# Convolution as 32x32 blocks on the array's diagonal, and router logits from four column tiles

## The reference

```python
xr = x @ in_proj_w.T
xs, res = jnp.split(xr, 2, axis=-1)
xc = conv_general_dilated(moveaxis(xs, 1, 2), conv_w, window_strides=(1,), padding=[(3, 0)],
                          feature_group_count=512)          # one 4-tap filter a channel
xs = silu(moveaxis(xc + conv_b[None, :, None], 2, 1))
dt, B, C = split(xs @ x_proj_w.T, ...)
delta = softplus(dt @ dt_proj_w.T + dt_proj_b)
y = selective_scan(xs, delta, -exp(A_log), B, C)            # h = exp(delta A) h + delta u B;  y = C h
x = x + ga * ((y * silu(res)) @ out_proj_w.T)
h = layernorm(x) * (1 + cb) + sb
s_raw = h @ Wg                                              # router logits, 8 a token
x = x + gb * moe(h, s_raw, Wl1, Wl2)
```

## Time and profile before

| | us |
|---|---|
| median of 3 runs | 2515.86 |
| lowest and highest | 2515.31, 2516.01 |
| span of the profiled execution | 2510.4 |
| mean granted TensorE clock in it | 0.902 |

### The profile page before, as it was taken

How to read it: one execution, slowest core, us unless ns; L and a number is a source line. 1 busy time by engine, 2 the same in 40 slices (tenths; PEclk the granted TensorE clock), 3 DMA queues, 4 the chain that set the end, 5 groups by cost and what they waited for, 6 DMA issues and landing times. The chain is left out here.

```text
span 2510.4 us, 31164 instructions
## 1 busy us (share of the span) xinstructions
PE 2181.1 (87%) x7664; PEld 1059.5 (42%) x7665; DVE 1929.5 (77%) x2060; ACT 1390.4 (55%) x2472; POOL 1955.0 (78%) x840
## 2 busy tenths in 40 slices
PE   8769998989989898999898988989857649999997
PEld 3214343443434343444343443434323335556654
DVE  2799899999999999989899999999897162222222
ACT  3666666667575766666666667576644232222221
POOL 1999889898989898989889898989897014555553
PEclk9878889898989898988989898989878869999999
DMA  5443242424232323434242424232321062222221
GB/s 155 129 112 96 73 102 66 100 71 112 79 94 73 97 76 95 107 85 102 73 102 67 101 69 114 80 92 77 91 68 39 26 208 77 85 84 82 87 85 45
DMA packets 149402, 224.40 MB, mean 89 GB/s; under 512 B 48227, under 2 KB 85617, under 8 KB 145138
## 3 DMA queue, kind: packets, MB, share of 16 engines
q1 hardware_dynamic: 135858, 182.44, 27.8%
q0 software_dynamic: 13376, 40.12, 5.1%
HBM read 99.48 MB, written 31.47 MB: 52 GB/s over the span
## 5 line engine op out<-in xcount | busy, mean ns | idle before, releaser
L1029 POOL TENSOR_TENSOR hs<-hs,c_rep 128x2048 f32<-128x2048 f32 x256 | 1154.8, 4532 | 41.3 <-ACT state L772 41.1
L869 DVE TENSOR_TENSOR_SCAN hs<-dA,state,hs 128x512 f32<-128x512 f32 x768 | 931.4, 1265 | 20.7 <-ACT dA L752 16.4
L752 ACT ACTIVATE dA<-d_rep,a 128x512 f32<-128x512 f32 x1024 | 688.8, 686 | 411.2 <-DVE hs L869 409.2
L1022 POOL TENSOR_TENSOR hs<-u_rep,b_rep 128x2048 f32<-128x2048 f32 x96 | 435.8, 4540 | 88.6 <-PE bank L516 88.5
L856 DVE TENSOR_TENSOR hs<-u_ps,b_rep 128x2048 f32<-128x2048 f32 x160 | 361.2, 2274 | 10.1 <-issue 5.1
L487 PE MATMUL bank<-n,w1s 128*128 128x512 f32 x512 | 269.0, 663 | 68.0 <-DVE delta L837 39.2
L869 DVE TENSOR_TENSOR_SCAN hs<-dA,hs 128x512 f32<-128x512 f32 x256 | 294.2, 1204 | 20.0 <-ACT dA L752 18.8
L516 PE MATMUL bank<-hs,spread 128*32 128x512 f32 x2048 | 280.4, 696 | 31.1 <-POOL hs L1029 27.0
L1414 DVE TENSOR_TENSOR hid<-z,sg 128x512 f32<-128x512 f32 x70 | 48.4, 692 | 298.2 <-ACT sg L1392 298.2
L1332 PE MATMUL z<-w1r,hT 128*128 x560 | 260.6, 608 | 3.5 <-issue 2.4
L445 PE MATMUL bank<-xin,w_in 128*128 128x512 f32 x512 | 246.3, 621 | 7.9 <-ACT xin L599 7.9
(11 more groups left out here) (174 smaller groups left out, 2566.3 us busy)
## 6 DMA issues: line engine op xcount, KB each, us to landing
d_rep<-delta SPq DMA_DIRECT2D x1024, 64.0 KB, 2.0
u_rep<-us SPq DMA_DIRECT2D x384, 64.0 KB, 2.0
b_rep<-bc_rows SPq DMA_DIRECT2D x64, 256.0 KB, 4.4
c_rep<-bc_rows SPq DMA_DIRECT2D x64, 256.0 KB, 7.8
xres<-in_x SPq DMA_DIRECT2D x16, 512.0 KB, 3.3
token_rows<-xpad SPq DMA_DIRECT2D x32, 256.0 KB, 2.4
token_rows<-xres SPq DMA_DIRECT2D x16, 512.0 KB, 2.9
xin<-in_x SPq DMA_DIRECT2D x15, 512.0 KB, 9.4
```

The source lines that it names most:

```text
L752: nc.scalar.activation(dA[:, u % ABANK, :], d_rep[:, q, :], ACT.Exp, scale=t["a"][:, u:u + 1]).then_inc(da_ready, 1)
L869: nc.vector.tensor_tensor_scan(hs[:, s % RING, g, :], dA[:, u % ABANK, :], hs[:, s % RING, g, :], state[:, u:u + 1] if m else 0.0, ALU.mul ...
L1022: nc.gpsimd.tensor_tensor(hs[:, s % RING], u_rep[:, i % UBUF, :].unsqueeze(1).to_broadcast([P, NG, T]), b_rep[:, par, :].rearrange("p (g t ...
L1029: nc.gpsimd.tensor_tensor(hs[:, s % RING, :, :], hs[:, s % RING, :, :], c_rep[:, par, :].rearrange("p (g t) -> p g t", g=NG), ALU.mult).th ...
```

## The change

The convolution no longer uses diagonal matrices of 128x128. Of a diagonal matrix only the 32x32 blocks on the diagonal are kept: `w_conv` becomes 32 columns wide, and each matmul has 32 rows and 32 columns. Tile position (32 r, 32 b) of the array takes rows 32 r of block b of `xpad` and writes partitions 32 b of bank r: a result bank then holds 32 channels of each of the four blocks, and the host permutes the weights behind it to that order (`held_by`). Two banks, r = j and j + 1, are computed at once: CV 0 does CV 0 and CV 1, CV 2 does CV 2 and CV 3, with 32 matmuls each (4 taps, 4 blocks, 2 rows of tiles), and both banks are taken first. CV 1 and CV 3 are empty on TensorE. All four blocks of `xs` are waited for. `conv_made` rises by one after the last matmul of each of the two banks, both at the end of the pair.

The logits get the router's weights, padded to 32 columns, as stationary operand, and `h2T` as the moving one, 128 columns for each token tile, with the four token tiles in four column tiles. The result, experts by tokens, is copied by ScalarE to `lgT` (item GL), turned by one transpose (item GT, on TensorE after B 0), and copied again to `lg` (GT in ScalarE's table, before B 1).

```diff
-            9: [(('GL', 0), -1), (('RB', 1), -1), (('SUM', 1), 0), (('B', 0), -1), (('B', 1), -1), ...
+            9: [(('GL', 0), -1), (('RB', 1), -1), (('SUM', 1), 0), (('B', 0), -1), (('GT', 0), -1), (('B', 1), -1), ...
-            10: [[(('E0', 0), 1), (('GL', 0), -1), (('L0', 0), 1), (('RB', 1), -1)], [], [(('B', 0), -1)], [(('B', 1), -1)]],
+            10: [[(('E0', 0), 1), (('GL', 0), -1), (('L0', 0), 1), (('RB', 1), -1)], [], [(('B', 0), -1)], [(('GT', 0), -1), (('B', 1), -1)]],
...
+                if kind == "CV":
+                    return convolve(j, c, f)
...
-                elif kind == "CV":
-                    pe.wait_ge(xs_ready, KI * f + j + 1)
-                    for k in range(KCONV):
-                        last = nc.tensor.matmul(ps_[:, :], t["w_conv"][:, j, k, :], xpad[:, j, k:k + T], start=(k == 0), stop=(k == KCONV - 1))
...
                 elif kind == "GL":
                     pe.wait_ge(h2T_ready, KD * f + KD)
-                    for tt in range(TT):
-                        for k in range(KD):
-                            last = nc.tensor.matmul(ps_[:, tt * NEXP:(tt + 1) * NEXP], h2T[:, k, tt * P:(tt + 1) * P], t["wg"][:, k, :],
-                                                    start=(k == 0), stop=(k == KD - 1))
+                    for k in range(KD):
+                        for tt in range(TT):
+                            last = nc.tensor.matmul(ps_[DS * tt:DS * tt + DS, 0:P], t["wg"][:, k, :], h2T[:, k, tt * P:(tt + 1) * P],
+                                                    start=(k == 0), stop=(k == KD - 1), skip_group_check=True, tile_position=(0, DS * tt))
+                elif kind == "GT":
+                    pe.wait_ge(lgT_ready, f + 1)
+                    last = nc.tensor.transpose(ps_[:, 0:P], lgT[:], t["ident"][:])
...
+            def convolve(j, c, f):
+
+                if j % 2:
+                    return
+                first = take_bank(pe, ("CV", j), c, f)
+                pe.sem_inc(held, 1)
+                second = take_bank(pe, ("CV", j + 1), c, f)
+                pe.sem_inc(held, 1)
+                pair = ((j, first), (j + 1, second))
+                hold(pe, xs_ready, KI * f + KI, held)
+                for k in range(KCONV):
+                    for b in range(KI):
+                        for r, ps_ in pair:
+                            rows = slice(DS * r, DS * r + DS)
+                            last = nc.tensor.matmul(ps_[DS * b:DS * b + DS, :], t["w_conv"][rows, b, k, :], xpad[rows, b, k:k + T],
+                                                    start=(k == 0), stop=(k == KCONV - 1), skip_group_check=True, tile_position=(DS * r, DS * b))
+                            if k == KCONV - 1 and b == KI - 1:
+                                last.then_inc(conv_made, 1)
...
                 elif kind == "GL":
+                    nc.scalar.activation(lgT[:], ps_[:, 0:P], ACT.Copy).then_inc(lgT_ready, 1)
+                elif kind == "GT":
                     if not (known(f) and f == 0):
                         act.wait_ge(logits_stored, 16 * f)
-                    nc.scalar.activation(lg[:], ps_[:, 0:TT * NEXP].rearrange("p (t e) -> p t e", t=TT), ACT.Copy).then_inc(logits_kept, 1)
+                    nc.scalar.activation(lg[:], ps_[:, 0:P].rearrange("p (t e) -> p t e", t=TT)[:, :, 0:NEXP], ACT.Copy).then_inc(logits_kept, 1)
...
-                    last = nc.vector.tensor_scalar(t["w_conv"][:, j, k, :], t["ident"][:], cw[:, j, k:k + 1], None, ALU.mult)
+                    last = nc.vector.tensor_scalar(t["w_conv"][:, j, k, :], t["gather"], cw[:, j, k:k + 1], None, ALU.mult)
```

More of the change, by code:

```diff
@@ L86, in fused_program @@
         hs = sb("hs", [P, RING, NG, T])
-        lg, gs = sb("lg", [P, TT, NEXP]), sb("gs", [P, 2, TT])
+        lg, lgT, gs = sb("lg", [P, TT, NEXP]), sb("lgT", [P, P]), sb("gs", [P, 2, TT])
         state = t["state"]
@@ L124, in fused_program @@
         logits_made, logits_kept, logits_stored = sem("logits_made"), sem("logits_kept"), sem("logits_stored")
+        lgT_made, lgT_ready = sem("lgT_made"), sem("lgT_ready")
         gate_in, gate_exp, gate_inv, gate_soft, gate_ready = sem("gate_in"), sem("gate_exp"), sem("gate_inv"), sem("gate_soft"), sem("gate_ready")
@@ L141, in fused_program @@
             8: [(('RS', 2), 1), (('RS', 3), 1), (('T2', 0), -1), (('T2', 1), -1), (('DT', 0), 1), (('DT', 1), 1), (('RB', 0), -1)],
-            9: [(('GL', 0), -1), (('RB', 1), -1), (('SUM', 1), 0), (('B', 0), -1), (('B', 1), -1), (('B', 2), -1), (('DB', 0), 1), (('B', 3), -1), (('DT', 2), 1)],
+            9: [(('GL', 0), -1), (('RB', 1), -1), (('SUM', 1), 0), (('B', 0), -1), (('GT', 0), -1), (('B', 1), -1), (('B', 2), -1), (('DB', 0), 1), (('B', 3), -1), (('DT', 2), 1)],
             10: [],
@@ L205, in fused_program @@
                  ("DT", 0), ("DT", 1), ("DB", 0), ("DT", 2), ("DT", 3), ("DB", 1), ("RS", 0), ("DB", 2), ("RS", 1), ("DB", 3), ("RS", 2), ("RS", 3)]
-        ACT_READS = ("T", "XS", "CV", "RS", "XP", "DT", "T2", "RB", "GL", "B")
+        ACT_READS = ("T", "XS", "CV", "RS", "XP", "DT", "T2", "RB", "GL", "GT", "B")
         made = {"T": turned, "XS": xs_made, "RS": res_made, "CV": conv_made, "XP": xdbl_made, "DT": dt_made, "DB": db_made, "SUM": y_ready, "OP": out_made,
-                "T2": turned2, "RB": back_made, "GL": logits_made, "B": b_made, "A": a_made, "Y": out2_made}
+                "T2": turned2, "RB": back_made, "GL": lgT_made, "GT": logits_made, "B": b_made, "A": a_made, "Y": out2_made}
         kept = {"T": hT_ready, "XS": xs_ready, "RS": res_pre, "CV": us_pre, "XP": xdbl_ready, "DT": abs_ready, "DB": delta_ready, "SUM": yg_ready, "OP": x1_ready,
-                "T2": h2T_ready, "RB": back_kept, "GL": logits_kept, "B": b_kept, "A": hid_ready, "Y": acc_ready}
+                "T2": h2T_ready, "RB": back_kept, "GL": lgT_ready, "GT": logits_kept, "B": b_kept, "A": hid_ready, "Y": acc_ready}
         many = {"T": KD, "XS": KI, "RS": KI, "CV": KI, "XP": 1, "DT": KI, "DB": KI, "SUM": KI, "OP": 2,
-                "T2": KD, "RB": 2, "GL": 1, "B": KI, "A": KI, "Y": 2}
+                "T2": KD, "RB": 2, "GL": 1, "GT": 1, "B": KI, "A": KI, "Y": 2}
         FRONT = ("T", "XS", "CV", "RS", "XP", "DT", "DB")
@@ L1437, in build @@
                 "w_in": sb("w_in", [P, KD, 2 * DI]), "w_x": sb("w_x", [P, KI, PROJ]), "w_dt": sb("w_dt", [DT_ROWS, DI]),
-                "w_out": sb("w_out", [P, KI, D]), "w_conv": sb("w_conv", [P, KI, KCONV, P]), "sa": sb("sa", [P, KD, BATCH]),
+                "w_out": sb("w_out", [P, KI, D]), "w_conv": sb("w_conv", [P, KI, KCONV, DS]), "sa": sb("sa", [P, KD, BATCH]),
                 "ca": sb("ca", [P, KD, BATCH]), "sb2": sb("sb2", [P, KD, BATCH]), "cb2": sb("cb2", [P, KD, BATCH]),
-                "w1s": sb("w1s", [P, KD, 2 * H]), "w2s": sb("w2s", [P, KI, D]), "wg": sb("wg", [P, KD, NEXP])}
+                "w1s": sb("w1s", [P, KD, 2 * H]), "w2s": sb("w2s", [P, KI, D]), "wg": sb("wg", [P, KD, DS])}
             fused_program(nc, ins, t, bc_dram, wout_dram, w2_dram, mod_dram, gb_dram, rows_dram, logits_dram)
@@ L1455, in laid_out @@
     c = np.ascontiguousarray
+    held_by = np.arange(DI).reshape(SPC, KI, DS).transpose(1, 0, 2).reshape(DI)
+    w_in = a["L0_attn_in_proj_w"].T
     return {
         "x": c(a["L0_attn_x"].reshape(BATCH * SEQ, D)),
[L1459 to L1464, removed]
+        "w_in": c(np.concatenate([w_in[:, :DI], w_in[:, DI + held_by]], axis=1)), "conv_w": c(a["L0_attn_conv_w"].reshape(KI, P, KCONV).transpose(1, 0, 2)),
+        "conv_b": c(a["L0_attn_conv_b"][held_by].reshape(KI, P).T),
+        "w_x": c(np.insert(a["L0_attn_x_proj_w"].T[held_by], DT_RANK, 0.0, axis=1)),
+        "w_dt": c(np.concatenate([a["L0_attn_dt_proj_w"].T, a["L0_attn_dt_proj_b"][None]])[:, held_by]),
+        "a_cols": c(a["L0_attn_A_log"][held_by].reshape(KI, SPC, DS, NF, NG).transpose(3, 2, 0, 1, 4).reshape(P, NSET * NG)),
+        "w_out": c(a["L0_attn_out_proj_w"].T[held_by]), "wg": c(np.pad(a["L0_ffn_Wg_DN"], ((0, 0), (0, DS - NEXP)))), "w1": c(a["L0_ffn_Wl1_ND2H"]), "w2": c(a["L0_ffn_Wl2_NHD"]),
         "c": c(a["L0_c"].reshape(BATCH, KD, P).transpose(2, 1, 0)), "wmod": c(a["L0_wmod"]),
```

## The result

| | before | after |
|---|---|---|
| median of the runs, us | 2515.14 (2510.93 to 2516.5) | 2519.18 (2517.29 to 2522.06) |
| ratio of the times | | 1.0021, 95% interval 1.0014 to 1.0029 |
| span of the profiled execution, us | 2510.4 | 2516.4 |
| mean granted TensorE clock in it | 0.902 | 0.874 |

What follows compares the result with a forecast made beforehand. VectorE's scan thread was taken to bound the kernel. Logits -28.5, second pair +49.5, prologue -4, tail -1.9 sum to +15.1 us; with span 2510.4 and 5.5 around it, 2531.0 us, range 2484 to 2556 (forecast's own range 2511 to 2552).

Steps and rivals of the forecast that it cites:

- Logits, chunks 1 to 15: Ahead of SUM 1: logits 1.2 us for 3.58, VectorE gains 1.9 us a chunk, 28.5 us in all.
- The shift of banks: The added transpose shifts later items' banks; one new neighbour pair, T 1 and XS 0, already ordered by `hT_ready`; no cost.
- Second pair: Convolution's CV 2 and CV 3, chunks 0 to 14: ScalarE waits, delaying `dA` for set 5; 3.3 us each, 49.5 lost.
- The free time: How long the convolution's second pair may run before VectorE waits for `dA` of set 5: 3.3 us.
- The pair's length: Time of the convolution's second pair: 3.75 us at full clock, 7.1 at half clock, 6.6 taken.
- an earlier fall: Clock falls in the hole after the first pair: OP 0 runs slowly and the second hole is 2 to 3 us.
- Rival (b): Clock falls late or returns within the second pair: 5.3 to 5.9 us, no change, 2512 to 2521 us; chance 0.13.
- First pair and eight tiles: Convolution's CV 0 and CV 1: eight tiles run beside each other, 3.75 us at full clock.
- Rival (c): Convolution's eight tiles don't run beside each other: 16 rounds, 100 us lost, +66, 2582 us; chance 0.08.
- Prologue: Before the first scan: faster convolution, the product goes behind XP, XP starts at 38; gain 4 us.
- Tail: Logits in one chain with the last hidden layer: gain 2.2 less 0.3, 1.9 us.
- The frame: Time around the profiled span, median 2515.86 against span 2510.4: 5.5 us, added to the forecast.

Runs made afterwards that it cites:

- logits_only: Kernel before with only the logits' half of the change (8 stationary columns in place of 32, `lgT` in a free part of `hid`), convolution as before: 2486.62 us.
- conv_only: Kernel before with only the convolution's half of the change (pairs of 32x32 blocks), logits as before: 2556.0 us.
- unpaired: Changed kernel with the 32x32 blocks computed bank by bank, four tiles at a time in place of eight, no wait for a second bank: 2497.06 us.
- order_only: Kernel before with SUM 1 queued ahead of transposed copy RB 1 on TensorE and RB 1's copy later on ScalarE, no new instruction: 2512.99 us.

## Why the prediction was off

The sum was +15.1 us and the span gave +6.0. The direction, the chain and the place were right, and the sizes were not. Step by step:

- **Logits, chunks 1 to 15: -28.5 forecast.** The times were nearly exact (1.08 us for 1.2, and a full 2.4 us from the logits to the end of SUM 1). The shift of banks was put at nothing: the prediction looks only at the one new neighbour pair, T 1 and XS 0, and only for its order, and its "nothing is late there" is about GpSimd's gate. But the added transpose makes B 1 take the bank that B 0 has just filled, and `logits_only` shows the return: 37.3 us gone at SUM 1 and at `dA` of set 10, 17.9 back (11.8 at set 11, 2.6 at set 13, 3.5 at SUM 2), all in chunks 1 to 14. Net it measured -18.7 there and -3.1 in chunk 15, -21.8. In the changed kernel what is not stall at set 5 is -30.3 (5.4 + 5.4 - 3.1 - 38.0), because, it seems, the stall also covers some 9 us of the other waits (in the change SUM 1's wait, the one at set 11 and SUM 2's are 4.5, 3.1 and 4.7 us below those of `logits_only`, and that for `u_ps` 3.1 above). That the term looks right there is chance: two errors that cancel.
- **Second pair: +49.5 forecast, 38.0 measured. This is the step that failed**, by 11.5 us. The free time was right: 3.3 us forecast, 3.2 measured (5.77 less 2.5). The pair's length was not: 6.6 us taken, 5.77 in the mean. The prediction has the clock fall in the hole or a little into the pair and stay down. It also names an earlier fall, with OP 0 slow and a second hole of 2 to 3 us, and that came (5.40 and 2.81 us in chunk 8); but it has no rise after it. In chunks 1 to 14 the trace shows a fall between 1.2 us before OP 0 and 0.6 us into it, a rise 3.0 to 6.2 us after OP 0's start, so that the pair begins at 2.4 GHz, and a second fall 0.4 to 2.6 us into the pair. Only chunk 0's pair ran at 1.2 GHz throughout. Rival (b), "falls late", at 0.13, describes this, with a pair of 5.3 to 5.9 us and 2512 to 2521 us; it deserved to be the forecast. In `conv_only` the same term was 45.9 us with nothing changed in the convolution but the time at which the fall comes, with pairs of 6.3 us in the mean, so 6.6 was nearer for the convolution alone than for both parts.
- **First pair and eight tiles: right.** 3.66 us in every chunk (3.75 forecast). Rival (c) is out.
- **Prologue: -4 forecast, -0.1 measured.** The product (L587) was said to go behind XP; it stands ahead of it in TensorE's queue, with the faster convolution as without it. And the clock fell in the second pair, so that the product took 5.58 us instead of 3.60 and ended at 42.0, where it ended before.
- **Tail: -1.9 forecast, -1.5 after the last scan.** Right.
- **The frame.** The prediction puts 5.5 us around the span. In every run whose span is on record it is 1.8 to 2.1 us (2518.41 for 2516.4 in the profiled execution of the change), so the profiled execution of before was probably some 3 us faster than its median; this is enough to explain why the spans differ by 6.0 and the medians by 4.0. The upper end of the forecast's own range comes to 2550.5 by its own terms, not 2552.
- **Check of the sum:** 15.1 - 11.5 (pair) - 1.8 (logits, -30.3 for -28.5) + 3.9 (prologue) + 0.4 (tail) = 6.1 us.

The Trainium skill (TensorEngine Tiling, Key Properties) has the rule that changing the tiling mode drains TensorE. The runs show no price for it: the first pair starts 3.57 us after the column-tiled SUM ahead of it (1022.77 to 1026.34, chunk 8), and so did the whole-array convolution before (1015.31 to 1018.88). No run has the same work with no change of mode, so what both may pay is not shown. By the Trainium skill (TensorE: Matmul & The Clock Gate, Part 3) a further tile adds about 4 ns. The trace agrees: 64 records on eight tiles take 3.66 us, and the 32 records of SUM on four take 3.64.

What stays open: why the clock falls at the moment it does. Its place moved by 2.8 us against the pair between two kernels (the change and `conv_only`, chunk 8) with the same items and the same idle times from SUM 3 on.

## What to carry to other kernels

Before trading TensorE time for a wait (two banks at once, a group for single blocks), ask who is copying the bank and what stands behind that copy in its queue: here 4.7 us of TensorE's time a chunk that nobody waited for (14.17 us, now 3.66 and 5.77) were bought with a wait of 2.5 us that VectorE paid, and moving one copy by one step took that wait away. A new item in an alternation of buffers shifts every later neighbour, so go through the pairs for time as well as for races. And price a gap on TensorE at both clocks, as a range whose ends are two forecasts, not as one value near an end.

## What was not expected of the hardware

- Work on 32x32 tiles did not always keep the clock at 2.4 GHz. In chunk 8 of `unpaired` it fell after 4 us of such work with TensorE busy all the time, and stayed down for 10 us (1020.83 to 1031.07), where the kernel before stayed at 2.4 GHz. In no pair that started at 1.2 GHz did it rise before the end (7.08 us). With three whole-array matmuls (2.74 us) ahead of the pair it stayed up in chunks 1 to 14.
- The same pair took 4.75 us in one kernel and 7.08 in another, by when the fall came.
- Starting a sum 0.94 us sooner at 1.2 GHz brought only 0.45 us, since the rise did not come sooner with it (`order_only`).
